# Linear attention with an FP4 feed-forward: the five parts of the output projection placed one by one among the last projections and output groups of a tile

## The reference

```python
q = relu((x @ Wq).reshape(b, s, 64, 64)) * SCALE
k = relu((x @ Wk).reshape(b, s, 64, 64))
v = (x @ Wv).reshape(b, s, 64, 64)
kv = einsum('bsid,bsjd->bsdj', k, v)         # contracted over i, the heads of one row
out = einsum('bsid,bsdj->bsij', q, kv)
q_norm = einsum('bsid,bsd->bsi', q, k.sum(axis=2))
attn = (out / (q_norm[..., None] + EPS)).reshape(b, s, 4096) @ Wo + bo
x = layernorm(x + attn)
gate, y = fp4_linear(x, w_gate), fp4_linear(x, w_up)
x = layernorm(x + fp4_linear(silu(gate) * y, w_down))
```

## Time and profile before

| | |
|---|---|
| median of 3 runs | 2255.24 us |
| the profiled execution's own time | 2258.28 us |
| its span, first to last instruction | 2256.5 us |
| mean granted TensorE clock | 0.983 |
| PE, DVE, ACT, POOL busy | 91%, 80%, 71%, 77% |
| one iteration in the middle of the run | 33.64 us |

### The profile page before, as it was taken

One profiled execution on the slowest core, in us unless ns is written; L12 is line 12 of the kernel. 1 busy time (PEld: TensorE's weight loads), 2 busy tenths in 40 slices (PEclk: granted clock), 3 DMA queues, 4 the chain that ended last, 5 costly groups with the idle time before them and its releaser, 6 DMA issues.

```text
span 2256.5 us, 89008 instructions
## 1 busy us (share of the span) xinstructions
PE 2053.0 (91%) x37963; PEld 1958.4 (87%) x37963; DVE 1809.7 (80%) x3487; ACT 1601.0 (71%) x3210; POOL 1727.8 (77%) x2384
## 2 busy tenths in 40 slices
PE   4899999999999999999999999999999999999985
PEld 3798998998898898998898898898898899899874
DVE  6778878878878878888887887887887887887874
ACT  4677777777777777777777777777777777777762
POOL 4587787787787787787788778778778778778772
PEclk9899999999999999999999999999999999999986
DMA  6466666666666766756756766766766766666661
GB/s 195 100 137 145 142 134 138 149 128 138 149 131 135 151 132 135 157 126 136 154 129 133 154 132 131 155 133 130 151 135 130 149 138 131 146 142 130 141 130 34
DMA packets 523218, 308.34 MB, mean 137 GB/s; under 512 B 275590, under 2 KB 497734, under 8 KB 522310
## 3 DMA queue, kind: packets, MB, share of 16 engines
q1 hardware_dynamic: 522822, 302.65, 62.4%
HBM read 17.38 MB, written 4.19 MB: 10 GB/s over the span
## 4 chain that ended last, share of the span: by engine, by line
PE 39%; DVE 31%; POOL 15%; ACT 7%; issue 5%; DMA 2%; SPq 0%; DVEq 0%; POOLq 0%; ACTq 0%
PE ps L409 15%; DVE k_acc L775 9%; PE ps L362 8%; PE ps L364 8%; PE ps L363 8%; POOL q_nat L1082 7%; DVE v_st L793 5%; POOL o_st L1092 4%; DVE q L810 3%; ACT q_nat L609 3%; DVE k_acc L786 3%; ACT v_st L541 3%; DVE x L867 2%; DVE o L828 2%; POOL small L1100 2%
## 5 line engine op out<-in xcount | busy, mean ns | idle before, releaser
L1092 POOL TENSOR_TENSOR o_st<-o,o_st 128x256 bf16<-128x256 f32 x1024 | 663.2, 680 | 100.4 <-ACT o_st L651 100.4
L1082 POOL TENSOR_TENSOR q_nat<-q,q_nat 128x512 bf16<-128x512 f32 x512 | 589.4, 1174 | 32.1 <-ACT q_nat L609 31.1
L828 DVE TENSOR_TENSOR o<-ps,rec 128x512 f32<-128x512 f32 x512 | 354.2, 692 | 263.9 <-POOL o_st L1092 257.2
L362 PE MATMUL ps<-v_st,q_bd 128*128 128x66 bf16 x4096 | 457.0, 199 | 67.7 <-DVE o L828 62.0
L362 PEld LDWEIGHTS ps<-v_st,q_bd 128*128 128x128 bf16 x4096 | 420.1, 114 | 86.9 <-DVE o L828 69.4
L363 PE MATMUL ps<-v_st,q_bd 128*128 128x66 bf16 x4096 | 454.7, 198 | 0.0
L364 PE MATMUL ps<-v_st,q_bd 128*128 128x66 bf16 x4096 | 453.3, 197 | 0.0
L651 ACT CAST o_st<-o 128x256 bf16<-128x256 f32 x1024 | 357.6, 402 | 117.8 <-DVE o L828 112.7
L363 PEld LDWEIGHTS ps<-v_st,q_bd 128*128 128x128 bf16 x4096 | 417.6, 116 | 0.4 <-issue 0.4
L364 PEld LDWEIGHTS ps<-v_st,q_bd 128*128 128x128 bf16 x4096 | 417.0, 115 | 0.0
L409 PE MATMUL ps<-w_o,o_st 128*128 128x128 bf16 x6144 | 377.5, 220 | 5.2 <-DMA o_st<-swap 5.2
(11 more groups left out here) (130 smaller groups left out, 5413.6 us busy)
## 6 DMA issues: line engine op xcount, KB each, us to landing
q_bd<-q_nat SPq DMA_DIRECT2D x256, 256.0 KB, 3.9
swap<-v_st SPq DMA_DIRECT2D x64, 576.0 KB, 5.2
v_st<-v_st SPq DMA_DIRECT2D x64, 576.0 KB, 6.1
v_st<-swap SPq DMA_DIRECT2D x64, 576.0 KB, 6.6
swap<-o_st SPq DMA_DIRECT2D x64, 512.0 KB, 4.9
o_st<-o_st SPq DMA_DIRECT2D x64, 512.0 KB, 7.4
o_st<-swap SPq DMA_DIRECT2D x64, 512.0 KB, 6.0
x_in<-in_L_attn_x SPq DMA_DIRECT2D x64, 64.0 KB, 5.9
```

The costliest lines, as they stand in the source:

```text
L362: nc.tensor.matmul(dst, lhs(0), rhs(0), start=True, stop=False)
L828: nc.vector.tensor_tensor(o32[:, g % OR, :].rearrange("p (s b e) -> p s b e", b=2, e=HALF), slot_cols(("out", g))[:, :, 0:PW].rearrange("p ...
L1082: last = nc.gpsimd.tensor_tensor(qnat[:, 1, a, :, e, :], src[:, a], qnat[:, 0, a, :, e, :], ALU.subtract)
L1092: last = nc.gpsimd.tensor_tensor(lo[:, :, a], src[:, a], hi[:, :, a], ALU.subtract)
```

## The change

Only PE's list changes. The first part of the output projection moves from behind group 5 to ahead of group 4, right behind q2; the second from behind the first to between groups 4 and 5; the third from behind group 6 to ahead of it, right behind q3; the fourth from behind group 7 to ahead of it. The fifth stays last.

```diff
                 project(t, "q", 2)
+                wo_part(t, 0)
                 out_group(t, 4)
+                wo_part(t, 1)
                 out_group(t, 5)
-                wo_part(t, 0)
-                wo_part(t, 1)
                 project(t, "q", 3)
+                wo_part(t, 2)
                 out_group(t, 6)
-                wo_part(t, 2)
+                wo_part(t, 3)
                 out_group(t, 7)
-                wo_part(t, 3)
                 wo_part(t, 4)
```

## The result

| | median | runs | mean iteration |
|---|---|---|---|
| before | 2255.11 us | 2254.7 to 2257.67 (4) | 33.63 us |
| changed | 2314.5 us | 2306.83 to 2320.15 (4) | 34.50 us |

The ratio is 1.0259, with a 95% interval from 1.0225 to 1.0293: the change makes the kernel 2.6% slower. The profiled execution of the changed kernel has a span of 2309.3 us, 52.8 us more than before. Before, 60 x 33.63; now (2200.23 - 130.14) / 60 = 34.50. So 60 x 0.87 = 52 us, nearly all of it, is lost in these 60 iterations, but not evenly. Before, all but a few took between 33.5 and 33.7 us. Now the shortest is 33.63, the median 33.99 and the longest 37.78, and the 14 iterations above 35 us hold 37 of the 52 us.

The account below looks back on a forecast made before the run. PE was taken as nearly full (31.66 of 33.64 us). A 34.27 us ring over POOL and the exchange, taken as 34.34, gave +43 us over 61 repetitions, +45 in all: 2300 us, range 2266 to 2330.

Parts of the forecast that it names:

- The sum: Whole kernel: +0.70 us per iteration over 61 repetitions, +43, with the first and last iterations +45 us, giving 2300 us.
- The gain: PE at group 5: no more wait for DVE's scale_o(3), 1.15 us per iteration if part 1 started at 1126.46.
- The first tie, the ring over POOL and the exchange: Part 1, group 5, norm_o(5), q_hi(2), POOL's q_lo(2) to o_lo(7), three DMAs, next part 1: 34.27 us against 33.64.
- W: The start of part 1 of the output projection on PE, from which the forecast counts times within an iteration.
- its 0.07 us for the spread: Landing of the exchange's DMAs: late ones stop PE, early ones give back little, so 34.34 taken instead of 34.27 us.
- The second tie, the start of v: ACT's v_hi(0) later behind v0; v3 waits about 1.0 us, landing 24.2 behind v0, iteration 34.1 to 34.3 us.
- W+9.91: PE's next v0, forecast to start 9.91 us behind the start of part 1, against 11.06 us before.
- 3 us of slack: DVE's chain to scale_o(3): 0.7 to 1.0 us later, with about 3 us of slack in front of group 5.
- a fall of the clock: PE: five of 31.66 busy us at half clock, 2.5 us more per iteration, 2450 us; chance 0.02.
- the main case: Whole kernel slower by the two ties, 2300 us, spanning 2270 to 2325; chance 0.71.
- The rival that went with the fit: Exchange of o_st is quick, part 1 does not wait, 2246 us; chance 0.09, of which the fit holds 0.02.

Follow-up runs that it names:

- Experiment 8: Changed kernel with q_hi(2) ahead of norm_o(4) and norm_o(5) in ACT's list; 2289.7 us, ratio 1.0134 to the kernel before.
- experiment 5: Changed kernel with the third DMA of o_st's exchange ahead of v's second DMA in SP's list; 2265.36 us, ratio 1.0038 to the kernel before.
- experiment 3: Changed kernel with 9 more matmuls of 128 columns per iteration right ahead of part 1's wait for the exchange; 2307.03 us.
- experiment 2: Against the changed kernel, output projection parts 1 and 2 put back behind group 5, parts 3 and 4 left moved; 2308.76 us, ratio 1.0233 to the kernel before.
- experiment 1: Against the changed kernel, parts 3 to 5 put back where they stood, parts 1 and 2 left moved; 2325.3 us, ratio 1.0286 to the kernel before.
- experiment 10: Kernel before with only POOL's x_bias moved ahead of x_back; 2241.19 us, ratio 0.9932 to the kernel before.
- 6: Kernel before with parts 1 and 2 moved on PE and o_st's third DMA ahead of v's second; 2251.9 us, ratio 0.9972.
- 9: Kernel of 6 with POOL's x_bias moved ahead of x_back; 2265.7 us, ratio 1.0035 to the kernel before.
- 11: Kernel of 9 with POOL's rstd_2 moved behind o_lo(1) and ACT's y behind o_hi(2); 2263.28 us, ratio 1.0029 to the kernel before.
- 12: Kernel of 6 with POOL's x_bias moved between o_lo(0) and q_lo(0); 2250.32 us, ratio 0.9972 to the kernel before.
- experiment 4: Changed kernel with the load of x_res behind the second DMA of o_st's exchange in SP's list; 2304.09 us.

## Why the prediction was right

**The time and the sign.** 2300 us was forecast, with 2266 to 2330, and 2314.5 measured. The sum had +45 us. The profiled execution shows +52.8, and the medians are 59.4 apart.

**The gain.** Right: the wait at group 5 is gone, as is the 1 us per iteration that it cost.

**The first tie, the ring over POOL and the exchange.** Right in size, in the mean. The forecast was 5.61 + 9.64 = 15.25 us from W to the end of `o_lo(7)` and 19.02 for the exchange. In the iteration shown it is 15.21, and from `o_lo(7)` to the landing it is 18.99 in the mean of 60. That the median iteration is only 33.99 shows what the mean is made of: the exchange took from 17.0 to 21.1 us, the early ones gave back nothing below 33.6, and the late ones made the loss. The forecast said this of late and early landings, but it counted with medians, and its 0.07 us for the spread was taken without a count. That the mean came out so near is in part luck. Experiment 8 shows that a part of it goes over `q_hi(2)`, experiment 5 that it goes over the landing, experiment 3 that PE has room in it.

**The second tie, the start of v.** Right as a mechanism: it costs 0.85 us alone (experiment 2), and its marks are there, `v_lo(0)` 0.8 us later and the wait at v3. It also acts through the landing, as I had written: in 31 of the 45 iterations it, and not POOL, held back the second DMA. Yet the runs can't tell the changed kernel from the one without this tie (experiment 1). Too large in one step: v3 waits 0.55 us, not 1.0, in part since v0 itself comes 0.2 later than W+9.91. The forecast missed that v0's slot hangs on `scale_o(6)` and so on POOL. Experiment 2 shows that the tie also closes over DVE's chain to `scale_o(3)`, for which I had given it 3 us of slack; that slack exists only where group 5 comes late, as in the changed kernel.

**The term that was mis-sized: the clock.** I took a fall of the clock as a rival of its own, for 5 busy us in every iteration, at 0.02, and priced it at nothing in the main case. It came in some iterations. Windows of the changed kernel, ahead of a landing for which PE waited 2.87 us, behind it, and an ordinary iteration (us, busy us of PE, PEld, DVE, ACT, POOL, granted clock, DMA share, GB/s):

```profile
1119.00:1122.40 3.40, 0.53 (x10) 0.36 (x7) 2.18 (x6) 2.71 (x7) 3.37 (x5) 0.95 1.03 231
1122.40:1126.00 3.60, 3.59 (x49) 3.60 (x50) 0.54 (x2) 0.00 (x0) 2.87 (x5) 0.57 0.11 25
1133.93:1167.86 33.93, 31.93 (x593) 30.31 (x594) 27.49 (x54) 24.30 (x51) 26.71 (x38) 1.00 0.64 137
```

PE was busy for 0.53 of 3.40 us, and then ran at 0.57 of its clock, mostly its lower level of 1.2 GHz. In these iterations W to the end of `o_lo(7)` is 16.6 to 16.7 us instead of 15.2. There are six of them in which part 1 itself was slowed, 6 x 1.5 = 9 us, which with 45 makes 54, against the 52.8 that the profile shows. The spread of the runs goes the same way: mean granted clock 0.981 and 0.980 in the runs of 2311.1 and 2306.8 us, 0.975 and 0.977 in those of 2317.9 and 2320.2. The rule of the Trainium skill's page "TensorE: Matmul & The Clock Gate", section "HAM oscillation — how this bites in real kernels", that waits for a DMA in a matmul loop bring back the slow clock, had more to say here than my 0.02: it held in six of the 60 iterations.

**The exchange and the page's fit.** The rival that went with the fit of the Trainium skill's page "DMA: Bandwidth & Descriptors", section "Anatomy of one DMA — SWDGE (gpsimd) path" (an estimate of 9.6 us for the exchange), fell: the three DMAs took 4.8, 6.9 and 6.0 us in the changed kernel. Experiment 5 shows that v's exchange beside them is a reason why the last two are longer than the first: with v's second DMA behind them the third takes 4.9 us. The second still takes 6.5, and what holds it there was not tried.

## What to carry to other kernels

Moving work ahead of a wait is free only if the work has no wait of its own: ask for the slack of the semaphore that it waits for, and count what is queued behind it on an in-order engine. Here work whose semaphore came 1.7 us ahead of it in the mean (25.33 and 23.65 behind v0), and sometimes at the last moment, was moved 2.75 us forward. Then follow what the delayed blocks feed, round to the moved wait itself: where the path closes, its full length is the new iteration, whatever each engine's busy share. And where a wait on a busy engine is to be shortened, look first at its releaser's list: 0.4 us of work that stood ahead of it on POOL was worth more (experiment 10) than any order of PE that was tried.

## What I had not expected of the hardware

The clock's answer to a wait of 2 to 3 us is not the same each time. Both of these are part 1 of the changed kernel behind a long wait (timeline):

```profile
1542.66 1.36 PE L409 MATMUL ps<-w_o,o_st 128*128 128x128 bf16 x21 [2.71 <-DMA o_st<-swap]
...
702.05 2.33 PE L409 MATMUL ps<-w_o,o_st 128*128 128x128 bf16 x21 [1.93 <-DMA o_st<-swap]
```

In the first the 21 matmuls are at once back to 56 ns each; in the second they take 2.3 us. Of the twelve steady iterations with a wait of 1.8 to 2.9 us, six ran slow behind it and six did not; in experiments 1, 3 and 8 it was six of eighteen. In the kernel before, which has no such wait in its steady part, the clock never fell there.

PE can stand idle in the middle of a block of equal matmuls, with no semaphore to wait for. In the kernels in which it hardly waits otherwise (5, 6, 9, 11 and 12), such gaps of up to 1.5 us add up to some 10 to 17 us over the steady part; in the kernel before and the changed one there are next to none. Whether a shortage of instructions is behind it, and whether the DMA traffic bears on that, was not tried.

DMAs of 512 and 576 KB within the core's memory took 4.2 to 9.2 us in the changed kernel, by what ran beside them, and an earlier issue was paid for by a longer flight (experiment 4).
